# Edge counts of a graph transformer: weights on ScalarE, unpacking on VectorE after the counts, the first layer norm among the counts

## The reference, cut to what matters

```python
    edge_index = jnp.stack([src, dst])
    xn = _layernorm(x, axis=-1)
    x = x + _L0_gnn_ref(xn, edge_index, ...) + _L0_mix_ref(xn[None], ...)[0]
```

## Time and profile before

| | us |
|---|---|
| median of 3 runs | 3155.37 (3152.49 to 3160.29) |
| the profiled execution, device time | 3152.18 |
| its span in the trace | 3150.4 |
| TensorE busy | 2760.7 (88% of the span) |
| VectorE busy | 1448.0 (46%) |
| ScalarE busy | 1045.6 (33%) |
| GpSimd busy | 744.1 (24%) |

### The profile page before, as it was taken

One profiled execution on the slowest core, in us unless ns is written; L12 is line 12 of the kernel. 1 busy time (PEld: TensorE's weight loads), 2 busy tenths in 40 slices (PEclk: granted clock), 3 DMA queues, 4 the chain that ended last, 5 costly groups with the idle time before them and its releaser, 6 DMA issues. The chain is left out here.

```text
span 3150.4 us, 48268 instructions
## 1 busy us (share of the span) xinstructions
PE 2760.7 (88%) x19973; PEld 2491.1 (79%) x19973; DVE 1448.0 (46%) x3565; ACT 1045.6 (33%) x1899; POOL 744.1 (24%) x315
## 2 busy tenths in 40 slices
PE   8698999996679999988799899989887899997497
PEld 7698999994338878988779899987566798795497
DVE  8926465654113234468633532315745464105633
ACT  0032245550003213239332433243434243443131
POOL 2324221110002412320425143323013241101221
PEclk9999999998798999999999999989998899999799
DMA  2022221005991112220112122211001121100111
GB/s 64 1 61 76 77 88 36 26 16 209 413 370 55 56 31 53 72 88 1 61 46 71 41 81 71 72 60 46 1 8 49 51 76 46 44 21 12 31 61 55
DMA packets 162252, 220.35 MB, mean 70 GB/s; under 512 B 21521, under 2 KB 141003, under 8 KB 162034
## 3 DMA queue, kind: packets, MB, share of 16 engines
q1 hardware_dynamic: 162034, 217.26, 20.7%
HBM read 215.31 MB, written 1.92 MB: 69 GB/s over the span
## 5 line engine op out<-in xcount | busy, mean ns | idle before, releaser
L47 PE MATMUL ps<-weights_r,buf_r 128*125 128x256 f32 (+2 forms) x3970 | 541.4, 288 | 27.9 <-POOL weights_r L253 13.9
L253 POOL TENSOR_TENSOR weights_r<-weights,head_weights_r 128x1536 fp32r<-128x1536 f32 (+1 forms) x78 | 271.6, 3482 | 1137.6 <-ACT head_weights_r L246 1137.6
L47 PEld LDWEIGHTS ps<-weights_r,buf_r 128*125 128x125 f32 (+1 forms) x3970 | 510.1, 188 | 32.2 <-POOL weights_r L253 14.9
L253 POOL TENSOR_TENSOR weights_r<-weights,weights_r 128x1536 fp32r<-128x1536 f32 (+1 forms) x79 | 272.3, 3446 | 1029.5 <-ACT weights_r L246 1029.5
L47 PE MATMUL ps<-xT_r,weights_r 128*128 128x376 f32 (+1 forms) x2100 | 346.7, 310 | 0.0
L47 PE MATMUL ps<-head_weights_r,buf_r 128*125 128x256 f32 (+1 forms) x2360 | 326.8, 284 | 0.0
L47 PEld LDWEIGHTS ps<-xT_r,weights_r 128*128 128x128 f32 x2100 | 314.3, 188 | 5.1 <-issue 3.3
L47 PEld LDWEIGHTS ps<-head_weights_r,buf_r 128*125 128x125 f32 x2360 | 302.9, 188 | 0.0
L47 PE MATMUL ps<-weights_r,xT_r 128*125 128x256 f32 x1680 | 232.6, 282 | 12.3 <-DVE buf_r L699 8.9
L246 ACT ACTIVATE head_weights_r<-weights 128x1536 fp32r<-128x1536 f32 (+1 forms) x78 | 114.4, 1466 | 342.4 <-PE ps L47 217.8
L47 PEld LDWEIGHTS ps<-weights_r,xT_r 128*125 128x125 f32 x1680 | 213.2, 187 | 14.3 <-issue 11.2
(11 more groups left out here) (331 smaller groups left out, 4353.2 us busy)
## 6 DMA issues: line engine op xcount, KB each, us to landing
expert_regions<-in_L_ffn_w SPq DMA_DIRECT2D x64, 576.0 KB, 14.4
expert_regions<-in_L_ffn_w SPq DMA_DIRECT2D x48, 768.0 KB, 15.6
weights<-in_L_mix_fc_w SPq DMA_DIRECT2D x24, 768.0 KB, 4.5
weights<-in_L_gnn_W SPq DMA_DIRECT2D x18, 768.0 KB, 4.5
weights<-in_L_ffn_W SPq DMA_DIRECT2D x12, 768.0 KB, 4.6
weights<-in_L_mix_w_mapT SPq DMA_DIRECT2D x9, 768.0 KB, 4.6
weights<-in_L_gnn_W_out SPq DMA_DIRECT2D x9, 768.0 KB, 4.5
weights<-in_L_mix_kqv_wT SPq DMA_DIRECT2D x9, 768.0 KB, 4.5
```

The lines of the kernel that those rows point to most:

```text
L47: mm = net.nc.tensor.matmul(ps, net.r(stationary(s, k)), net.r(moving(m, k)), start=(n == 0 and k == 0), stop=(stop and n == 2 and k == kc ...
L253: self.nc.gpsimd.tensor_tensor(self.r(load.dst), load.dst, self.r(load.high), ALU.subtract).then_inc(self.low_made, 1)
```

## The change

1. In the counts VectorE no longer multiplies: it writes the one-hot row of the source (`src`, L1420) and that of the destination (`dst`, L1423). A new ScalarE instruction for each chunk multiplies `hot_src` in place by `value` (L1381), and TensorE waits for both engines.
2. Every flushed tile has a buffer of its own (25 `packed` tiles, in free parts of large buffers). Nothing is unpacked during the counts.
3. The statistics of the first layer norm, its root and its five products stand among the chunks 64 to 138. The root (after chunk 102 in ScalarE's queue) follows the wait for constants and the first two `split_high`, which are moved there from the head of the queue.
4. `ToFeatures` starts tile by tile, right behind the last counting matmul; the first linear starts tile by tile too (`tiles=features.made`).
5. A new stage `EdgeUnpack` does all unpacking and adding on VectorE, behind `ToFeatures` and ahead of the first `HeadNorm`. GpSimd does nothing of it. The third linear and the first `HeadNorm` wait for it.
6. `SelfLoops` moves behind the second `HeadNorm`.

The diff, cut (`...` marks what is left out):

```diff
-    def __init__(self, net, after=None):
+    AHEAD = 2
+
+    def __init__(self, net, x, out, eps, after=None):
...
+        rooms = [(g[5], 0, 12), (g[2], 960, 9), (net.P1, SLOT, 4)]
+        self.packed = [buf[:TP, o + 314 * k:o + 314 * k + w].bitcast(I32) for buf, o, n in rooms for k in range(n)]
...
+        first = 2 * self.FLUSH
+        extra = {first + 6 * t: [("stats", t, 0), ("stats", t, 1), ("mean", t)] for t in range(NT)}
+        extra[3 * self.FLUSH + 16] = [("inverse",)]
+        extra.update({3 * self.FLUSH + 18 + 6 * t: [("norm", t)] for t in range(NT)})
+        for c in range(self.CH):
+            dve += [("src", c), ("dst", c)] + extra.get(c, [])
+            act.append(("value", c))
+            f, j = divmod(c - self.AHEAD + 1, self.FLUSH)
+            if f > 0 and j < NT:
+                act += [("flush", f - 1, j)] + ([("flush", f - 1, 1)] if j == 0 else []) if j != 1 else []
+            if f == 3 and j == NT:
+                act.append(("root",))
+        act += [("flush", self.flushes - 1, t) for t in range(NT)]
...
-            pe.wait_ge(dve.sem, self.hot_made(c))
+            pe.wait_ge(self.net.act.sem, self.at["act"]["value", c])
+            pe.wait_ge(self.net.dve.sem, self.at["dve"]["dst", c])
...
+            if q[0] == "value":
+                hot = self.hot_src[q[1] % self.DEPTH][:, 0:self.HALF_SRC + 1]
+                act.wait_ge(self.net.dve.sem, dve["src", q[1]])
+                ins = nc.scalar.activation(hot, hot, ACT.Identity, scale=self.value[:, q[1]:q[1] + 1])
...
+            else:
+                act.wait_ge(self.net.const_landed, 16 * len(self.net.consts))
+                for u in range(2):
+                    self.net.split_high(u, 0)
+                act.wait_ge(self.net.dve.sem, dve["mean", NT - 1])
+                ins = nc.scalar.activation(self.rstd, self.net.mv[:, :, 1], ACT.Sqrt, bias=self.net.eps[self.eps][:TP, :])
...
+class EdgeUnpack(Stage):
+    side = True
...
+        for n, (f, t) in enumerate(tiles):
+            self.order += [("upper", f, t), ("lower", f, t)]
+            if n > 0 and tiles[n - 1][0] > 0:
+                self.order += [("add_lower", *tiles[n - 1]), ("add_upper", *tiles[n - 1])]
...
+            if kind == "upper":
+                dve.wait_ge(*self.edges.flushed[f][t])
...
+                ins = nc.vector.tensor_scalar(whole[:, w:N] if f == 0 else high, packed[:, 0:N - w], 12, None, ALU.logical_shift_right)
+            elif kind == "lower":
+                dve.wait_ge(done.sem, done.issued)
+                ins = nc.vector.tensor_scalar(whole[:, 0:w] if f == 0 else packed, packed, self.edges.RADIX - 1, None, ALU.bitwise_and)
+            elif kind == "add_lower":
+                dve.wait_ge(done.sem, self.at["lower", f, t])
+                ins = nc.vector.tensor_tensor(total[:, 0:w], whole[:, 0:w], packed, ALU.add)
+            else:
+                ins = nc.vector.tensor_tensor(total[:, w:N], whole[:, w:N], high, ALU.add)
...
-    norm_T(net, R, tok(G[0]), XT, 1e-5)
-    loops = SelfLoops(net, ALU.add, start + edges.ends())
+    features = ToFeatures(net, tok(G[0]), XT, after=[], tiles=edges.normed)
+    unpack = EdgeUnpack(net, edges, features.ends())
...
-    linear(net, XT, w, tok(G[1]), cols=(D, 2 * D), evac="a")
-    made = now()
+    linear(net, XT, w, tok(G[1]), cols=(D, 2 * D), evac="a", tiles=features.made)
+    made = now() + unpack.ends()
...
     linear_T(net, XT, w, feat(G[0]), cols=(0, D), evac="a", after=start)
+    loops = SelfLoops(net, ALU.add, unpack.ends())
```

More of the change, by code:

```diff
@@ L1335, in tile_done @@
         return self.p0 + f * self.per + self.FLUSH - 1 + t + 1
[L1337 to L1351, removed]
     def tensor(self, pe):
         self.begin(pe)
-        done, dve = self.net.pe, self.net.dve
+        done = self.net.pe
         for c in range(self.CH):
             f, j = divmod(c, self.FLUSH)
-            pe.wait_ge(dve.sem, self.hot_made(c))
+            pe.wait_ge(self.net.act.sem, self.at["act"]["value", c])
+            pe.wait_ge(self.net.dve.sem, self.at["dve"]["dst", c])
             for t in range(NT):
@@ L1379, in gpsimd @@
-    def gpsimd(self, pool):
-        self.begin(pool)
-        nc, done, w = self.nc, self.net.pool, self.HALF_SRC
-        for f in range(self.flushes):
-            for t in range(NT):
-                counts = self.net.counts[:TP, t, :].bitcast(I32)
-                pool.wait_ge(self.net.dve.sem, self.unpacked(f, t))
-                for part, c0, n in ((self.packed[:, t], 0, w), (self.high[t], w, N - w)):
-                    if f == 0:
-                        ins = nc.gpsimd.tensor_copy(counts[:, c0:c0 + n], part[:, 0:n])
-                    else:
-                        ins = nc.gpsimd.tensor_tensor(counts[:, c0:c0 + n], counts[:, c0:c0 + n], part[:, 0:n], ALU.add)
-                    ins.then_inc(done.sem, done.one())
-        for t in range(NT):
-            counts = self.net.counts[:TP, t, :]
-            pool.wait_ge(done.sem, self.l0 + 2 * (NT * (self.flushes - 1) + t) + 2)
-            nc.gpsimd.tensor_copy(counts, counts.bitcast(I32)).then_inc(done.sem, done.one())
@@ L1397, in unpack @@
[L1397 to L1405 removed]
+        nc, done, dve = self.nc, self.net.act, self.at["dve"]
@@ L1416, in vector @@
-        nc.vector.tensor_scalar(self.upper, self.idx[:, 0], float(self.HALF_SRC), None, ALU.is_ge).then_inc(done.sem, done.one())
-        dve.wait_ge(done.sem, done.issued)
-        nc.vector.scalar_tensor_tensor(out=self.folded, in0=self.upper, scalar=-float(self.HALF_SRC), in1=self.idx[:, 0],
-                                       op0=ALU.mult, op1=ALU.add).then_inc(done.sem, done.one())
-        nc.vector.tensor_scalar(self.value, self.upper, float(self.RADIX - 1), 1.0, ALU.mult, ALU.add).then_inc(done.sem, done.one())
```

143 lines of the change are left out of this document (89 added, 54 removed).

## The result

The changed kernel takes 3119.69 us (median of 4 runs, 3112.95 to 3122.07), beside 3153.93 for the kernel before on the same chip: ratio 0.9884, 95% interval 0.9863 to 0.9906. It is faster by 34 us; the forecast was 3128, and the range (3116 to 3141) holds the result. It lies in the band that the prediction gave to rival 1 (3115 to 3123, chance 0.25), not in that of the forecast (3124 to 3132, 0.45). The profiled execution took 3121.55; its span is 30.7 us shorter than that of before (3150.4), where the forecast said 27.4.

A forecast was written before the change was run, and what follows sets the result against it. VectorE was taken to bound the later flushes' counts and the time until the transposes. Gains of 14.5 and 20.1 us less losses of 7 and 0.2 gave 27.4, taking the median from 3155.4 to 3128; range 3116 to 3141.

The forecast's parts named there:

- rival 1: Unpacking beside the linears: additions cost the plain price, it ends by 49 us after the first linear's start; 3121, chance 0.25.
- first matmul: Start of the counts: after the first source row, ScalarE's table load and first multiplication, TensorE begins at 11.1 us.
- slow start: Start of the counts: TensorE's first matmuls run at half pace on a cold clock, a loss of 2.5 us.
- wait at the root: Counts, after chunk 102: TensorE waits 3.7 us for ScalarE, busy with flush copies, two splits, table load and root.
- half clock behind it: Counts, after the root's wait: TensorE likely runs at half the clock, 2.4 us more; from below, nothing.
- from there to the first linear: Last count to first linear: 3.4 us in place of 23.5, a gain of 20.1 us.
- one custom addition, start to start: VectorE's unpacking: each of 30 integer additions over 626 half words priced at 0.76 us, 22.8 in all.
- unpacking ends: VectorE beside the linears: unpacking ends at S + 62.4 us, S being the first linear's start; five GpSimd splits fall in.
- delay of the head norms: Behind the unpacking: the keys' `HeadNorm` comes 5 to 8 us late, taken as 7, passed on in full.
- hidden locks: Counts, after the root: GpSimd's two low parts lock VectorE out until T + 12.6, T in the third flush; costs TensorE nothing.
- the self-loops: `SelfLoops` falls into VectorE's idle time during the fourth linear, after the second `HeadNorm`, at a price of 0.2 us.
- signs of being wrong: Listed as refuting the prediction: TensorE waits at each flush or chunk, additions far from 0.8, keys' square at its old distance.

The follow-up runs named there:

- norm_behind: The changed kernel with the first layer norm put behind the counts again, the unpacking staying beside the linears: 3117.3 us, ratio 0.9888.
- adds_38: The changed kernel with 38 additional integer additions of 313 columns in the unpacking, results unused: 3134.0 us, ratio 0.9933.
- weights_on_vector: The changed kernel with the sources' multiplication back inside VectorE's comparison and none on ScalarE: 3116.0 us, ratio 0.9878.
- splits_apart: The changed kernel with ScalarE's two weight splits and the root taken apart in its queue: 3111.6 us, ratio 0.9865.
- combined: The changed kernel with multiplication inside VectorE's comparison, ScalarE's splits and root apart, and the ones set behind the first head norm: 3113.4 us, ratio 0.9871.
- apart_ones: The changed kernel with ScalarE's splits and root apart and the ones set behind the first head norm, multiplications staying on ScalarE: 3108.4 us, ratio 0.9851.

## Why the prediction was right, and which term was not

| step of the prediction | forecast | measured |
|---|---|---|
| first matmul | 11.1 | 11.15 |
| slow start, on top of 0.1325 a matmul | 2.5 | 3.6 (515 in 71.85 us) |
| wait at the root | 3.7 | 3.63 |
| half clock behind it | 2.4 | 3.1 (285 in 40.85 us); 0.3 in three other executions |
| last count | 125.7 | 127.5 |
| from there to the first linear | 3.4 | 3.4 |
| one custom addition, start to start | 0.76 | 0.39 |
| unpacking ends | S + 62.4 | S + 43.6 |
| delay of the head norms | 7 | 0 |
| gain | 27.4 | 32.8 at 255 us, 30.7 at the end |

**The counts.** Bound, wait and the hidden locks were right. The pace was a little short: the fastest stretches took 0.1335 us a matmul (285 in 38.05 us), 0.8 us more over 800, and 16.0 us by 121 is 0.132 and not 0.1325. Against this pace the slow start costs 3.1 us and the half clock 2.8, so each term was about half a microsecond short. The 2.4 also had luck in it, as three executions of the same counts show next to nothing there. The slow start itself (8, 10 and 10 matmuls in the first three stretches of 2 us from 11.2) stands at a granted clock given as 1.00, so that it is the clock is not shown. A gain of 12.8 us stands in place of 14.5.

**To the first linear.** 20.1 us were forecast, and 20.1 were measured (23.5 less 3.4). The prediction read the whole wait of 16.2 us as the layer norm; by the rows 6.9 of it was the unpacking of the last flush. The norm's 9.3 vanish because VectorE's lead on TensorE grew to 7.2 us, not because the norm was moved (norm_behind). The remaining 3.9 are the tile-by-tile start and the self-loops.

**The mis-sized term** is "hence 0.83 long and 0.76 from start to start" for the custom additions. I scaled by the listed columns, 626 half words, from another custom instruction. They take 0.39, as the plain additions of the same data do, so the work is 12 us and not 23, and with it three of GpSimd's splits fall in and not five. The square of the keys therefore still waits for ScalarE, with 13.4 us to spare (183.42 to 196.81), and the loss of 7 us is not there: rival 1, which forecast 3121. Two of the prediction's own signs of being wrong came true, additions far from 0.8 and the square of the keys at its old distance from S (S + 65.9, before 229.63 less 163.72, the same), and TensorE's wait for the split stayed at 8.0 where 15 was expected. So the range held the result, but the mechanism of the loss did not happen.

**What followed from it** was right in direction: with an unpacking of S + 65.4 (adds_38) the delay appears, is passed on in full, and grows from 8.3 to 13.3 us by other splits. Additions as priced would have ended the unpacking 3 us earlier, at S + 62.4. From this I estimate a delay of 5.3 us, and of 10.3 if the same stretching followed: 3125 to 3130. No run shows it.

**The sum** then reads 12.8 + 20.1 - 0 - 2.2 = 30.7 us in place of 14.5 + 20.1 - 7 - 0.2 = 27.4. The forecast came within 3.3 us because 7.2 us too much loss stood against 1.7 too much gain and 2.2 given back that no term had.

**The self-loops** were costed at 0.2 us in VectorE's idle time. That holds only while `SetOnes` holds the split back: the first instruction group there takes 7.57 us for five, from 251.34 on, beside two splits, but TensorE waits until 255.15 and then has the fourth linear to do. With `SetOnes` early, TensorE waits 6.4 us at the summary, against 0.8 with the self-loops elsewhere.

**Given back.** That an equal wait of 2.0 us is followed by a lower clock in one kernel and not in the other stood in no step. It goes with the loss of 2.2 us; why it falls in the one and not in the other stays open. The changed kernel's runs lie 9 us apart; that the clock is the cause there too is not shown: only the profiled execution has a trace, and the mean granted clock is 0.950 at 3112.95 us as at 3122.07.

**The two rules.** The table loads at the first multiplication (9.20) and at the root (84.54) take 1.28 us, and the next instruction starts 0.02 later. The Trainium skill ("ScalarE: Activation LUTs", What ACT_TABLE_LOAD costs) adds a drain of 1.38 us; the trace does not agree. The Trainium skill's rule that multiplications belong on VectorE (same page, Rules for kernel authors) is borne out for the single instruction: the multiplication costs VectorE 0.054 us a chunk, ScalarE 0.45. In time these runs don't decide it. The counts did not get longer, weights_on_vector is not clear of noise, splits_apart takes the root's wait away with the multiplication on ScalarE, and combined, with it on VectorE, was no faster than apart_ones.

What stays open: how much of the 3.7 us between the medians of weights_on_vector and the changed kernel is the edit, since the same counts scatter by as much (the 285 matmuls by 2.8 us).

## What to carry to other kernels

Price an unseen instruction from both sides, and let its data decide as much as its listed columns; what then matters is where the slack ends, which the last row before an idle stretch shows. When a stage shrinks, undo its parts one at a time, and read beside it what stood there before: here moving the norm gave nothing, since taking the unpacking away had already given VectorE the time for it. Work put into an engine's idle time is free only as long as the wait that makes the time idle is there, and a shift of a few microseconds changes which instructions stand beside GpSimd's splits. A forecast that comes out near can still rest on a loss that isn't there; its signs of being wrong tell it.

## What the runs showed of the hardware

- A custom integer addition over 626 half words and a plain one over 313 words take VectorE the same 0.48 us (0.39 to 0.40 from start to start). A ScalarE multiplication of 314 half-precision columns by a value per partition takes 0.56, 0.45 from start to start.
- The same wait of 3.63 us in the same code was followed by 285 matmuls in 38.05 to 40.85 us, with a granted clock of 0.71 or of 1.00 in the ten microseconds behind it.
- Beside a split of GpSimd (3.4 to 3.8 us) VectorE's instructions of 0.38, 0.48 and 4.16 us took 3.55, 3.78 and 7.35. Not every one does: the sum over 3840 columns at 174.66 took its usual 4.15 beside a split that began at 175.66. It goes the other way too: a split that began at 217.89, 0.8 us into a product on VectorE (217.08, 4.16 us), took 6.73.
